# The one-hot matrices of near edges: VectorE's TENSOR_SCALAR comparisons written as TENSOR_TENSOR, in the last message pass of a graph network

## The chip, the cores and the metric

One core of a Trainium2 chip runs the whole program. The metric is the device time of one execution, in microseconds; the median of three runs of the kernel before is 5305.56 us (5305.24 to 5307.98).

## What is computed

A stack of four graph layers over 6250 nodes of 256 features and 100,000 edges; `dst` is sorted, `src` is random. Only the fourth layer, a graph convolution, matters here:

```python
h = jnp.maximum(_layernorm(x, axis=-1), 0.0)
# edge_index = stack([src, dst]); row = src, col = dst
dinv_sqrt = jnp.where(deg > 0, jax.lax.rsqrt(deg_safe), 0.0)
w = dinv_sqrt[row] * dinv_sqrt[col]
h = jax.ops.segment_sum(w[:, None] * x[col], row, num_segments=N)   # x here is the layer's input h
h = h @ W + b
return x + jnp.where(h >= 0, h, LEAKY_ALPHA * h)
```

The destinations are drawn as the square of a uniform number, so many edges point to the first nodes.

## The kernel before, in words

The nodes are in 49 buckets of 128 (NB). A message pass takes 128 edges at a time, a tile: POOL gathers 128 rows of a table in HBM by an indirect DMA (one instruction a tile), VectorE builds a one-hot matrix that says to which row of the bucket each edge belongs, and TensorE multiplies the matrix with the gathered rows and so sums them in PSUM.

The last pass is `bucket_pass` (L1539) with the name gcn. Its table `htab` holds the layer's input, already scaled. It treats edges in two ways. Edges whose `dst` is 640 or more ("rest") go by gathers, at most 12 tiles a bucket, 586 in all. Edges whose `dst` is one of the first 640 nodes ("near", DEEP = 5 blocks of 128) are not gathered: those 640 rows stay in SBUF (`rows`), and the pass counts how often each node of the bucket has an edge to each of them. For that, VectorE makes two one-hot matrices of each of at most 6 near tiles of a bucket, in `near_hot`: `hot_to` (L1609, 128 columns, which node of the bucket) and `hot_of` (L1610, 640 columns, which near row), 293 of each, written as bf16 from fp32 constants `iota` and `wide`. TensorE multiplies them in `near_sum` (L1664, up to 30 matmuls of 128x128, into `psA`), ScalarE copies the counts to `times` (L1639), and `near_product` (L1674) multiplies them with `rows` into the bucket's sum.

Each engine runs a list of its own, written out by hand; k is the place of a tile in its bucket b.

- POOL (L1591): gather t into slot t mod 16 of `got`, after the sum of tile t - 16 is done (`sums`).
- VectorE: the one-hot of the gathered tile 8 places ahead (L1601, `tensor_scalar`, fp32), then at k = 2 to 7 the near matrices of bucket b + 1 (one pair each), then the steps of the bucket before: at k = 8 `y` = product + bias (L1491, waits for TensorE's product of k = 6), at k = 9 the leaky slope (L1495), at k = 10 the sum with x (L1498).
- TensorE: the tile's matmul (L1682), after k = 1 `near_sum(b)`, after k = 6 `near_product(b)`; at k = 3 the transposes (L1526) and at k = 6 the product with the weights (L1532) of the bucket before.
- ScalarE: at k = 1 the scaled copy `a` of the finished bucket (L1508), at k = 3 `times` of bucket b, at k = 4 the copy of the transposes (L1512), at u = 11 the store of the result (L1515).

`near_hot(b)` waits for `near_sum(b - 2)` (two buffers); `near_sum(b)` waits for all near matrices up to bucket b (`near_hots`). Other lines that the text names: L765, in the attention pass (`edge_pass`), is a multiplication of VectorE with both inputs in SBUF, one of them broadcast along the free dimension; L1760 is the gather of the edge network, whose VectorE steps (L1783, L1802) have one input in PSUM; L577 scatters records and L1135 gathers them for the lists of edges.

Of the kernel before, what the change touches and what calls it, by code (L numbers as in the profile page):

```python
# [19 lines left out]
ALU = mybir.AluOpType  # L20
ACT = mybir.ActivationFunctionType
AX = mybir.AxisListType
P = 128
# [24 lines left out]
DEEP = 5  # L48
# [67 lines left out]
def wait_count(eng, sem, count):  # L116

    if count is not None and not (isinstance(count, int) and count <= 0):
        eng.wait_ge(sem, count)
# [1155 lines left out]
class Behind:  # L1275
# [10 lines left out]
    def sb(self, name, shape):  # L1286
        return self.st.enter_context(self.nc.sbuf_tensor(f"{name}_behind_{self.nm}", shape, F32))
# [4 lines left out]
    def sem(self, name):  # L1292
        return self.nc.alloc_semaphore(f"{name}_behind_{self.nm}")
# [245 lines left out]
def bucket_pass(nc, c, nm, table, row_of, rel_of, lay, behind, near=None):  # L1539
# [7 lines left out]
    with ExitStack() as st:  # L1547
# [8 lines left out]
        if near is not None:  # L1556
            to, of, rows_d = near
            layn = c.layouts["near"]
            first_near = [sum(layn.counts[0:b]) for b in range(NB + 1)]
            wide = sb("wide", [P, DEEP * P])  # L1560
            hot_to, hot_of = sb("hot_to", [P, 2, NEAR, P], BF16), sb("hot_of", [P, 2, NEAR, DEEP * P], BF16)
            times, rows = sb("times", [P, 2, DEEP, P]), sb("rows", [P, DEEP, D])
            psA = [[pt(f"psA{q}{h}") for h in range(2)] for q in range(2)]
            near_hots, near_sums, times_made, near_made, rows_in, widened = [sem(x) for x in (
                "near_hots", "near_sums", "times_made", "near_made", "rows_in", "widened")]
# [6 lines left out]
        @block.sync  # L1572
        def _(sp):
            if near is not None:
                sp.dma_start(rows[:, :, :], rows_d[0:DEEP * P, :].rearrange("(k p) d -> p k d", p=P)).then_inc(rows_in, 16)
                sp.wait_ge(rows_in, 16)
            for i in range(NB):
                after.keep(sp, i)
            after.sync_end(sp)
# [14 lines left out]
        @block.vector  # L1594
        def _(dve):
            def one_hot(t):

                if t >= lay.n:
                    return
                wait_count(dve, sums, t - U + 1)  # L1600
                nc.vector.tensor_scalar(hot[:, t % U, :], c.iota[:, :], rel_of[:, t:t + 1], None, ALU.is_equal).then_inc(hots, 1)  # L1601

            def near_hot(b, i):

                if near is None or b >= NB or not 0 <= i < layn.counts[b]:
                    return
                t = first_near[b] + i
                wait_count(dve, near_sums, b - 1)
                nc.vector.tensor_scalar(hot_to[:, b % 2, i, :], c.iota[:, :], to[:, t:t + 1], None, ALU.is_equal)  # L1609
                nc.vector.tensor_scalar(hot_of[:, b % 2, i, :], wide[:, :], of[:, t:t + 1], None, ALU.is_equal).then_inc(near_hots, 1)  # L1610

            after.vector_start(dve)
            if near is not None:
                dve.wait_ge(widened, 1)
                for i in range(NEAR):
                    near_hot(0, i)
            for t in range(HOT_LEAD):
                one_hot(t)
            for t, (b, k) in enumerate(where):
                one_hot(t + HOT_LEAD)  # L1620
                near_hot(b + 1, k - 2)
                if b:
                    after.vector(dve, b - 1, k)
                if k == lay.counts[b] - 1:
                    for u in range(k + 1, max(steps, U)):
                        if b:
                            after.vector(dve, b - 1, u)
            for u in range(max(steps, U)):
                after.vector(dve, NB - 1, u)
            after.vector_end(dve)  # L1630
# [1243 lines left out]
```

## Time and profile before

| | |
|---|---|
| median of three runs | 5305.56 us |
| the profiled execution, its span | 6597.1 us |
| TensorE busy (matmul) | 3895.4 us, 59% |
| VectorE busy | 2562.6 us, 39% |
| ScalarE busy | 1792.3 us, 27% |
| POOL busy | 3799.2 us, 58% |
| granted TensorE clock | 0.714 of full speed |
| last pass (gcn), in the profile | 5715 to 6597 us |

The profile is of one execution, whose time is its span; nothing is recorded around it. It is longer than every timed run: durations of single instructions and the order of events are read from it, and how they carry over to the runs has to be argued. Busy shares are means over stages with different limits, so each stage is read by itself.

### The profile page before, as it was taken

What the parts mean: (1) busy time and instruction counts of PE and PEld (TensorE: products, weight loads), DVE (VectorE), ACT (ScalarE), POOL (GpSimd) and SP (SyncE); (2) the same over time, 40 slices, a digit from 0 to 9 for tenths busy, and PEclk for the clock granted to TensorE, in tenths of its full rate; (3) what the DMA queues carried; (4) which work ended last, traced back from release to release, by engine and by line L of the source; (5) the groups of instructions that cost most, each with busy time, mean ns of one, the idle gap of its engine ahead of it and who ended that gap; (6) DMA issues with size and microseconds to landing.
All of it is one profiled execution on the core that took longest, in us unless ns stands there. A gap on an engine that the chain in (4) does not pass through costs nothing. (4 is left out here: it accounts for less than half of the span.)

```text
span 6597.1 us, 65618 instructions
## 1 busy us (share of the span) xinstructions
PE 3895.4 (59%) x14913; PEld 2594.0 (39%) x14914; DVE 2562.6 (39%) x8644; ACT 1792.3 (27%) x5648; POOL 3799.2 (58%) x3942
## 2 busy tenths in 40 slices
PE   4232666667641533596455555566777777577777
PEld 2121333333320510242333333355566555455555
DVE  4223444444430300132222222255555555644443
ACT  0111555555530400011000000044444444400000
POOL 3554666666666077402666666666666666277776
PEclk7565666766665765796676666667777777688888
DMA  1011332332310010144433333323333333233332
GB/s 48 20 41 60 88 88 87 89 89 87 88 45 3 0 42 22 59 148 141 124 99 98 98 98 98 96 82 87 87 87 86 87 86 89 77 98 99 99 98 87
DMA packets 277662, 527.83 MB, mean 80 GB/s; under 512 B 80566, under 2 KB 175259, under 8 KB 277049
## 3 DMA queue, kind: packets, MB, share of 16 engines
q0 software_dynamic: 176144, 422.24, 22.5%
q1 hardware_dynamic: 85200, 86.14, 3.9%
q10 hardware_dynamic: 15960, 15.41, 0.7%
q8 instruction: 137, 2.24, 0.1%
q14 instruction: 221, 1.81, 0.1%
HBM read 433.63 MB, written 89.82 MB: 79 GB/s over the span
## 5 line engine op out<-in xcount | busy, mean ns | idle before, releaser
L675 POOL DMA_INDIRECT got_attend_src_dst<-dram_gtab,gather_src x832 | 800.4, 962 | 531.0 <-DVE msg_attend_src_dst L747 320.9
L577 POOL DMA_INDIRECT dram_rec_src<-rec_src x784 | 766.5, 978 | 509.6 <-issue 243.5
L1760 POOL DMA_INDIRECT got_edge_mlp_src_dst<-dram_ptab,gather_src x832 | 786.3, 945 | 463.2 <-DVE pre_edge_mlp_src_dst L1802 252.9
L1591 POOL DMA_INDIRECT got_rgcn<-dram_xtab,gather_of_type x831 | 788.3, 949 | 392.5 <-issue 187.9
L1886 PE MATMUL psS_edge_mlp_src_dst<-msg_edge_mlp_src_dst,hot_edge_mlp_src_dst 128*128 128x256 f32 x1664 | 736.1, 568 | 434.0 <-DVE sage_sums L1783 223.6
L1591 POOL DMA_INDIRECT got_gcn<-dram_htab,gather_rest x586 | 616.5, 1052 | 234.1 <-issue 148.9
L861 PE MATMUL psS_attend_src_dst<-msg_attend_src_dst,hot_attend_src_dst 128*128 128x264 f32 x1664 | 700.8, 513 | 19.5 <-DVE msg_attend_src_dst L747 14.3
L2091 PE MATMUL psO_tab<-w_tab,hT_tab 128*128 128x512 f32 (+1 forms) x980 | 474.4, 633 | 350.1 <-issue 200.5
L1886 PEld LDWEIGHTS psS_edge_mlp_src_dst<-msg_edge_mlp_src_dst,hot_edge_mlp_src_dst 128*128 128x128 f32 x1664 | 388.5, 269 | 589.7 <-issue 338.8
L1682 PE MATMUL psS_rgcn<-got_rgcn,hot_rgcn 128*128 128x257 f32 x1662 | 543.8, 471 | 79.7 <-DMA got_rgcn<-dram_xtab,gather_of_type 55.0
L1783 DVE TENSOR_TENSOR sage_sums<-sage_sums,psS_edge_mlp_src_dst 128x256 f32 x832 | 347.8, 418 | 523.6 <-PE psS_edge_mlp_src_dst L1886 246.1
L884 PE MATMUL psF_attend_src_dst<-ident,hot_attend_src_dst 128*128 128x128 f32 x832 | 314.4, 378 | 356.2 <-ACT hotT_attend_src_dst L832 190.4
L877 PEld LDWEIGHTS psN_attend_src_dst<-node,hotT_attend_src_dst 128*128 128x128 f32 x1664 | 412.5, 253 | 138.1 <-issue 41.4
L1682 PEld LDWEIGHTS psS_rgcn<-got_rgcn,hot_rgcn 128*128 128x128 f32 x1662 | 362.8, 234 | 237.3 <-issue 169.2
L2091 PEld LDWEIGHTS psO_tab<-w_tab,hT_tab 128*128 128x128 f32 x980 | 199.3, 215 | 573.1 <-issue 409.3
L1850 ACT ACTIVATE msg_edge_mlp_src_dst<-pre_edge_mlp_src_dst 128x256 f32<-128x256 f32 x832 | 340.3, 413 | 293.8 <-DVE pre_edge_mlp_src_dst L1802 211.3
L1802 DVE TENSOR_TENSOR pre_edge_mlp_src_dst<-got_edge_mlp_src_dst,psE_edge_mlp_src_dst 128x256 f32<-128x256 f32 x832 | 344.4, 414 | 158.4 <-remote 104.1
L709 DVE TENSOR_TENSOR sums<-sums,psS_attend_src_dst 128x264 f32 x832 | 350.7, 422 | 64.8 <-issue 31.5
L861 PEld LDWEIGHTS psS_attend_src_dst<-msg_attend_src_dst,hot_attend_src_dst 128*128 128x128 f32 x1664 | 361.1, 266 | 37.2 <-DVE msg_attend_src_dst L747 30.7
L1601 DVE TENSOR_SCALAR hot_rgcn<-iota,rel_src 128x128 f32<-128x128 f32 x831 | 216.9, 315 | 390.4 <-remote 180.5
L2067 DVE COPY out_tab<-psO_tab 128x512 f32<-128x512 f32 x196 | 133.7, 690 | 588.4 <-DMA got_edge_mlp_src_dst<-dram_ptab,gather_src 308.9
L1682 PE MATMUL psS_gcn<-got_gcn,hot_gcn 128*128 128x257 f32 x1172 | 322.8, 409 | 64.8 <-issue 30.8
(397 smaller groups left out, 5878.7 us busy)
## 6 DMA issues: line engine op xcount, KB each, us to landing
dram_xtab<-out_tab SPq DMA_DIRECT2D x48, 1024.0 KB
got_edge_mlp_src_dst<-dram_ptab,gather_src POOLq DMA_INDIRECT x832
got_attend_src_dst<-dram_gtab,gather_src POOLq DMA_INDIRECT x832
got_rgcn<-dram_xtab,gather_of_type POOLq DMA_INDIRECT x831
dram_rec_src<-rec_src POOLq DMA_INDIRECT x784
got_gcn<-dram_htab,gather_rest POOLq DMA_INDIRECT x586
dram_gtab<-sums ACTq DMA_DIRECT2D x48, 132.0 KB
x_sb<-x_in SPq DMA_DIRECT2D x1, 6144.0 KB
```

Of the source, the lines that this page charges most:

```text
L577: nc.gpsimd.indirect_dma_start(edges.to, bass.IndirectOffsetOnAxis(edges.rec[:, column, PLACE:PLACE + 1].bitcast(I32), 0), edges.rec[:, co ...
L675: nc.gpsimd.indirect_dma_start(got[:, t % U, 0:w], None, table, bass.IndirectOffsetOnAxis(row_of[:, t:t + 1], 0)).then_inc(row_in[t % U], 16)
L709: nc.vector.tensor_tensor(here, here, psS[t[1] % banks][:, 0:cols], ALU.add).then_inc(added, 1)
L861: nc.tensor.matmul(psS[t[1] % banks][:, 0:cols], hot[:, t[1], :], rows(t), start=True, stop=True).then_inc(sums, 1)
L877: nc.tensor.matmul(psN[t[1] // 2 % 2][:, 2 * HEADS * (t[1] % 2):2 * HEADS * (t[1] % 2 + 1)], hotT[:, t[1] % 4, :], c.node[:, :, :].rearran ...
L1591: nc.gpsimd.indirect_dma_start(got[:, t % U, 0:D], None, table, bass.IndirectOffsetOnAxis(row_of[:, t:t + 1], 0)).then_inc(row_in[t % U], 16)
L1682: nc.tensor.matmul(psS[b % 2][:, 0:D + 1], hot[:, t % U, :], got[:, t % U, 0:D + 1], start=(k == 0), stop=(k == lay.counts[b] - 1), skip_g ...
L1760: nc.gpsimd.indirect_dma_start(got[:, t % U, 0:width], None, table, bass.IndirectOffsetOnAxis(row_of[:, t:t + 1], 0)).then_inc(row_in[t % ...
L1783: nc.vector.tensor_tensor(here, here, psS[t[1] % banks][:, 0:cols], ALU.add).then_inc(added, 1)
L1802: nc.vector.tensor_tensor(pre[:, t[1] % 4, :], got[:, t[1], 0:D], psE[t[1] % 4][:, 0:D], ALU.add).then_inc(pres, 1)
L1886: nc.tensor.matmul(psS[t[1] % banks][:, 0:cols], hot[:, t[1], :], msg[:, t[1] % 8, :], start=True, stop=True).then_inc(sums, 1)
L2091: last = nc.tensor.matmul(psO[(NBK * t[1] + b) % 4][:, 0:z - a], hT[:, t[1], k * P:(k + 1) * P], w[:, k, a:z], start=(k == 0), stop=(k == 1))
```

## The change

In `near_hot` both comparisons become `tensor_tensor` with the column of indices broadcast along the free dimension. The values are the same; sizes, types, order, waits and the semaphore stay. The one-hot of the gathered tiles (L1601) stays a `tensor_scalar`.

```diff
--- before.py
+++ after.py
@@ -1606,8 +1606,9 @@
                     return
                 t = first_near[b] + i
                 wait_count(dve, near_sums, b - 1)
-                nc.vector.tensor_scalar(hot_to[:, b % 2, i, :], c.iota[:, :], to[:, t:t + 1], None, ALU.is_equal)
-                nc.vector.tensor_scalar(hot_of[:, b % 2, i, :], wide[:, :], of[:, t:t + 1], None, ALU.is_equal).then_inc(near_hots, 1)
+                nc.vector.tensor_tensor(hot_to[:, b % 2, i, :], c.iota[:, :], to[:, t:t + 1].to_broadcast([P, P]), ALU.is_equal)
+                nc.vector.tensor_tensor(hot_of[:, b % 2, i, :], wide[:, :], of[:, t:t + 1].to_broadcast([P, DEEP * P]),
+                                        ALU.is_equal).then_inc(near_hots, 1)
 
             after.vector_start(dve)
             if near is not None:
```

## Rows read from the trace of the kernel before

**Rows 1.** The last stage: length, busy PE, PEld, DVE, ACT, POOL, clock, DMA, GB/s.
```profile
5715.00:6597.00 882.00, 635.11 (x3421) 496.99 (x3421) 366.97 (x1319) 75.53 (x196) 617.23 (x588) 0.83 0.32 96
```

**Rows 2.** Groups by line in 5715 to 6597: busy us, mean ns, idle before.
```profile
L1591 POOL DMA_INDIRECT got_gcn<-dram_htab,gather_rest x586 | 616.5, 1052 | 234.1 <-issue 148.9 <-PE psS_gcn L1682 42.9 <-DMA got_attend_src_dst<-dram_gtab,gather_src 42.3
```

**Rows 3.** Groups by line of the whole span, POOL's; then POOL's longest single wait.
```profile
L675 POOL DMA_INDIRECT got_attend_src_dst<-dram_gtab,gather_src x832 | 800.4, 962 | 531.0 <-DVE msg_attend_src_dst L747 320.9 <-issue 190.7 <-POOLq L2751 19.4
L1591 POOL DMA_INDIRECT got_rgcn<-dram_xtab,gather_of_type x831 | 788.3, 949 | 392.5 <-issue 187.9 <-PE psS_rgcn L1682 102.4 <-remote 101.6
L1760 POOL DMA_INDIRECT got_edge_mlp_src_dst<-dram_ptab,gather_src x832 | 786.3, 945 | 463.2 <-DVE pre_edge_mlp_src_dst L1802 252.9 <-issue 210.3
L577 POOL DMA_INDIRECT dram_rec_src<-rec_src x784 | 766.5, 978 | 509.6 <-issue 243.5 <-POOLq L2751 211.5 <-PEq L1943 37.5
...
POOL rows_order_whole L1135 <- SPq L1117: 320.0, 1, 320.0
```

**Rows 4.** The timeline of one bucket: start us, us, engine, line, idle before.
```profile
6103.23 1.84 PE L1664 MATMUL psA_gcn<-hot_to_gcn,hot_of_gcn 128*128 128x128 bf16 x30
6103.24 0.29 DVE L1601 TENSOR_SCALAR hot_gcn<-iota,rel_rest 128x128 f32<-128x128 f32 x1
6103.44 0.28 DVE L1609 TENSOR_SCALAR hot_to_gcn<-iota,rel_near 128x128 bf16<-128x128 f32 x1
6103.63 0.54 DVE L1610 TENSOR_SCALAR hot_of_gcn<-wide_gcn,near_dst 128x640 bf16<-128x640 f32 x1
6103.78 1.44 POOL L1591 DMA_INDIRECT got_gcn<-dram_htab,gather_rest  x1 [0.31 <-issue]
6104.10 0.28 DVE L1601 TENSOR_SCALAR hot_gcn<-iota,rel_rest 128x128 f32<-128x128 f32 x1
...
6105.53 1.41 POOL L1591 DMA_INDIRECT got_gcn<-dram_htab,gather_rest  x1 [0.30 <-issue]
...
6112.05 0.76 ACT L1639 COPY times_gcn<-psA_gcn 128x512 f32<-128x512 f32 x2 [9.01 <-remote]
6112.33 0.94 POOL L1591 DMA_INDIRECT got_gcn<-dram_htab,gather_rest  x1 [1.35 <-DMA got_attend_src_dst<-dram_gtab,gather_src]
...
6112.86 4.11 PE L1674 MATMUL psS_gcn<-rows_gcn,times_gcn 128*128 128x256 f32 x10 [2.98 <-issue]
...
6116.81 1.03 PE L1532 MATMUL psO_behind_gcn<-w,aT_behind_gcn 128*128 128x256 f32 x4
...
6117.67 3.20 PE L1682 MATMUL psS_gcn<-got_gcn,hot_gcn 128*128 128x257 f32 x14
6117.87 0.42 DVE L1491 TENSOR_TENSOR y_behind_gcn<-psO_behind_gcn,bias 128x256 f32<-128x256 f32 x1 [10.08 <-issue]
...
6118.40 0.42 DVE L1495 SCALAR_TENSOR_TENSOR z_behind_gcn<-y_behind_gcn 128x256 f32<-128x256 f32 x1
6118.58 1.07 POOL L1591 DMA_INDIRECT got_gcn<-dram_htab,gather_rest  x1 [0.30 <-PE psS_gcn L1682]
6118.74 0.28 DVE L1601 TENSOR_SCALAR hot_gcn<-iota,rel_rest 128x128 f32<-128x128 f32 x1
...
6120.70 1.84 PE L1664 MATMUL psA_gcn<-hot_to_gcn,hot_of_gcn 128*128 128x128 bf16 x30
```

**Rows 5.** The waits in 5715 to 6597; then one window of PE's near_product.
```profile
ACT times_gcn L1639 <- remote: 348.5, 44, 17.6
...
6112.86:6117.00 4.14, 4.14 (x11) 3.37 (x12) 0.00 (x0) 0.22 (x1) 3.23 (x4) 0.59 0.30 93
```

**Rows 6.** The attention pass: VectorE's L765 by line, then the timeline.
```profile
L765 DVE TENSOR_TENSOR sums<-sums,own 128x1792 f32<-128x1792 f32 x7 | 13.6, 2018 | 2.3 <-issue 2.3
...
4308.60 3.95 DVE L765 TENSOR_TENSOR sums<-sums,own 128x1792 f32<-128x1792 f32 x2
4309.80 1.64 POOL L675 DMA_INDIRECT got_attend_src_dst<-dram_gtab,gather_src  x1 [0.30 <-issue]
```

## The prediction, made before the changed kernel was run

> **What bounds the kernel now.** I read the stages first, then the fourth pass by line, then one bucket of it in order of time.
>
> Stages [rows 1]: the change touches the last stretch alone, 5715 to 6597 us, 882 us for 49 buckets and 586 gathers. POOL is busy there for 617 us and PE for 635, DVE for only 367. So VectorE has slack, and its longer work costs nothing by itself; what counts is what it does to POOL.
>
> By line [rows 2]: in this pass a gather takes 1052 ns on average. In the relational pass the same instruction takes 949 and in the edge network 945 [rows 3]. The excess is 586 x 0.107 = 63 us, and no PE or DMA row explains it.
>
> In order of time [rows 4]: a gather with VectorE quiet takes 0.94 us and the next one starts 0.30 later, a spacing of 1.25. While VectorE makes near matrices they take 1.44 and 1.41. The second value repeats, since VectorE goes round a step of three comparisons in 0.854 (6103.24 to 6104.10), and a gather with its gap takes two such steps, 1.71 (6103.78 to 6105.53 is 1.75, the one before it not yet in step). So POOL and VectorE exclude each other somewhere, and POOL loses. Beside L1495, too, a gather takes 1.07.
>
> What else waits: PE's 30 near_sum matmuls are over by 6105.07, yet ScalarE, which waits for their semaphore alone, copies at 6112.05. PE sits idle at near_product for 3 us meanwhile, and POOL, 16 tiles ahead, idles 1.35 instead of 0.30 [rows 4]. One bucket's loop there is PE's: 8.8 from near_sum's first matmul to the copy, 0.8 copy, 4.1 near_product, 1.0 product, 3.2 for seven tiles, some of it overlapped, and near_sum starts again 17.5 us after it did. No operation of the program accounts for those 7 us, and `remote` is all that the view of the waits names for them, 348 us in the pass [rows 5]. The span is 6597.1 and the median of the runs 5305.56, 20% less. I take the late semaphore for something of the profiled execution. POOL's own spacing must be shorter in the runs as well: 832 + 832 + 831 + 586 + 784 = 3865 such instructions x 1.25 = 4831 us, and with two waits in which POOL does nothing (320 us at L1135, 212 at L577) this is 5363, over the median [rows 3]. So in the runs a gather's spacing s is below 1.25; it is not under 0.945, what the instruction itself takes. **I choose** s of 1.0 to 1.2, and POOL as the bound of the pass: 12 gathers per bucket are 12 to 14.4 us, while PE's work with prompt semaphores is 12 tiles x 0.457 (seven take 3.20) + 1.8 for near_sum + 4.1 for near_product, or half of that at full clock (it ran at a granted 0.59 [rows 5]), + 1.7 for the two products of the bucket before = 11 to 13.
>
> **The change part by part.** It replaces 293 comparisons of 128 columns and 293 of 640, one for one; no semaphore, queue or DMA moves.
> - VectorE's time. TENSOR_SCALAR: 0.196 from start to start for 128 columns, 0.463 for 640, so 0.52 ns a column over 0.13. TENSOR_TENSOR: 256 columns take 0.418 with the next start after 0.336 [rows 4], 1792 columns 2.018 with the next after 1.93 [rows 6], so 1.04 ns a column over 0.07. Two fp32 inputs in SBUF thus cost 0.20 for 128 columns and 0.736 for 640 (durations about 0.285 and 0.82). The step grows from 0.854 to D = 0.196 + 0.202 + 0.736 = 1.134, VectorE's busy time by 293 x 0.28 = 82 us. The cover: VectorE idles 10 us per bucket before L1491 [rows 4], the burst of six steps grows by 1.7, and the near matrices are due a bucket later. If a bucket takes 13 us in the runs there are still some 4 us. I cost it at nothing; without cover it is those 82 us.
> - POOL's loss today: 63 us of excess in the profile, less 49 x 0.12 = 6 for the gather of 1.07: 57 us, 1.2 per bucket. With a shorter spacing the same burst costs between that and three gathers x (1.71 - s), 2.1 at s = 1.0.
> - POOL's loss afterwards. No row shows a 640-column TENSOR_TENSOR beside this gather. Lowest bound: none, as beside additions that read PSUM, where the 832 gathers of the edge network average 945. Upper bound: the gather stands still as it does now, for the longer 0.736. The nearest row is L765 [rows 6], a multiplication with two SBUF inputs, 2.02 us each. A gather started at 4309.80 under one that ran from 4308.60 to 4310.62, and ended at 4311.44, 0.82 after it: its normal 0.95 counted from 0.13 before its end. So such an instruction does hold a gather **that wants to start**, until about 0.13 before its recorded end. The next L765 had begun at 4310.53 and did not stop it again. That is the difference from today, where a gather is stopped at its start and again later, by the next 640-column comparison. From this I price the new loss: at a random moment the start waits (0.82 - 0.13)^2 / (2 x 1.134) = 0.21, with the short comparisons 0.23; a burst of 6.8 us holds 4.6 gathers at s = 1.25, 1.06 us per bucket, 52 us in all. If s is under 1.134, the gathers fall in step with VectorE, one a step, and lose 6 x (1.134 - s): 0.2 at s = 1.1, 0.8 at 1.0.
> - The sum. s = 1.25: 57 - 52 = 5 us won. s = 1.1: 3 x 0.61 = 1.8 before, 0.2 after, 1.6 per bucket, 78 us. s = 1.0: 1.0 (out of step, like now) to 2.1 before against 0.8, so 0.2 to 1.3 per bucket, 10 to 64 us. Not all of it reaches the end, since PE's loop is close behind. I take 0.5 us per bucket, 49 x 0.5 = **25 us**. Against the profile's own 6597.1 the same terms give 5 us, and there PE's late loop hides them; a profile after within 10 us of that span would not contradict me.
>
> The Trainium skill, SBUF — State Buffer, "Who interferes with whom", says that a two-port VectorE instruction shuts GpSimd out, that tensor_tensor with two SBUF inputs contends only with GpSimd instructions that read SBUF, and infers that descriptor generation, which writes, is not held by it. By that all 57 us would come back. The gather of 1.64 us [rows 6] speaks against it for the start and for it afterwards.
>
> **The rivals.**
> - *Nothing that can be measured* (within 0.2%, 10.6 us, about what a measurement of this kernel can tell). Either s is near 1.2, where the two losses are alike, or PE's loop bounds the runs as it does the profile: then POOL's relief becomes a longer wait for sums. For: the 1.35 idle and the 17.5 us loop. Against: the loop needs the 7 us semaphore delay. 5300 to 5306.
> - *Full relief*: TENSOR_TENSOR does not hold the gathers at all. For: the 945 of the edge network. Against: [rows 6]. All 57 us: 5249.
> - *Slower*: the longer hold outweighs the second stop. Place: the start of each gather in a burst. Price: 6 x (D - s) per bucket against 1.0 to 1.2 now. It decides from D - s of 0.2, so with s near 1.0 if the comparisons' overhead is the 0.13 of TENSOR_SCALAR (D = 1.26) and not 0.07: 1.5 against 1.0, 0.5 x 49 = 25 us, 5331.
> - *The change does nothing to the instruction*: the broadcast column could be taken as a scalar again. L765 has such an operand and stands in the trace as TENSOR_TENSOR at 1.04 ns a column [rows 6]; I count this with the first rival, at 5306.
>
> **How the numbers follow.** Forecast 0.42, nothing measurable 0.28, full relief 0.09, slower 0.21. Time: 5305.6 - 25 = 5281. Range: down to the sum at s = 1.1 less a few us, 5232; up to most of the slower case, 5325. Both signs hold much of the chance; the forecast's own range is 5232 to 5294. Faster 0.42 + 0.09 = 0.51, same 0.28, slower 0.21.
>
> **What the profile after would show.** Right: L1609 and L1610 as TENSOR_TENSOR of about 285 and 820 ns, a step of 1.13, a mean gather under 1052 but over 945, with its excess in gathers that start under a L1610 and none in those that start just after one. Wrong: a mean of 945 (full relief), or over 1052 (slower); an idle before L1491 near zero, which would make VectorE the bound; or gathers relieved and POOL's wait for sums grown by as much, which would make it PE's pass.

## The result and the profile after

The changed kernel takes 5362.63 us (median of 4 runs, 5361.77 to 5363.98) against 5306.25 of the kernel before in the same session: a ratio of 1.0104 with a 95% interval of 1.009 to 1.0119, 56 us slower. The forecast was 25 us faster, with a range that ended at 5325.

First, the profile shown ahead of the prediction has to be set right. The profile of the changed kernel spans 5360.1 us, what its runs take. The kernel before, profiled once more (experiment e1), spans 5313.6 and not 6597.1. The first profile was of a disturbed execution. What its instructions take on VectorE and POOL was true all the same; what it showed of TensorE's late semaphores was not of this kernel. The comparison below is therefore of the profile after with the second profile of before.

The kernel before, second profile: the first line of the page, POOL's group of the last pass, the last pass as one window (length, busy PE, PEld, DVE, ACT, POOL, clock, DMA share, GB/s), and its longest waits.

```profile
span 5313.6 us, 65614 instructions
...
L1591 POOL DMA_INDIRECT got_gcn<-dram_htab,gather_rest x586 | 619.6, 1057 | 178.5 <-issue 97.7 <-PE psS_gcn L1682 80.8
...
4495.00:5313.00 818.00, 617.21 (x3421) 451.29 (x3421) 366.02 (x1319) 78.43 (x196) 620.36 (x588) 0.93 0.34 103
...
PE psS_gcn L1682 <- DMA got_gcn<-dram_htab,gather_rest: 130.3, 207, 1.7
```

The same of the changed kernel, with the page's line of engines.

```profile
span 5360.1 us, 65614 instructions
...
PE 3836.6 (72%) x14909; PEld 2402.2 (45%) x14914; DVE 2673.2 (50%) x8644; ACT 1795.6 (33%) x5648; POOL 3860.8 (72%) x3942
...
L1591 POOL DMA_INDIRECT got_rgcn<-dram_xtab,gather_of_type x831 | 789.8, 950 | 253.4 <-issue 159.6
...
L1591 POOL DMA_INDIRECT got_gcn<-dram_htab,gather_rest x586 | 673.6, 1150 | 178.4 <-issue 112.3 <-PE psS_gcn L1683 66.1
...
4489.00:5360.00 871.00, 649.94 (x3421) 487.64 (x3421) 444.94 (x1319) 78.44 (x196) 674.38 (x588) 0.87 0.33 97
...
PE psS_gcn L1683 <- DMA got_gcn<-dram_htab,gather_rest: 176.2, 173, 2.0
```

In both profiles POOL's idle time in the pass is 178 us, and that is no wait: 586 x 0.30 us between two gathers. It is 178 us in the profile of every experiment below too, whatever TensorE and VectorE did there. So POOL never waits for another engine there; it **is** the pass. Its busy time grew from 619.6 to 673.6, by 54 us, the pass by 53, the run by 56. TensorE waits for the gathers' data, 130 us before and 176 after; the mean granted clock of the pass is 0.93 before and 0.87 after, and since POOL does not wait for TensorE, that is not what made the pass longer. The relational pass, whose gathers took 949 ns before [rows 3], is at 950: the loss is all in the last pass.

VectorE's side of it, the changed kernel by line (busy us, mean ns, idle before):

```profile
L1610 DVE TENSOR_TENSOR hot_of_gcn<-wide_gcn,near_dst 128x640 bf16<-128x640 f32 x293 | 237.8, 812 | 0.0
...
L1609 DVE TENSOR_TENSOR hot_to_gcn<-iota,rel_near 128x128 bf16<-128x128 f32 x293 | 81.5, 278 | 6.4 <-POOL wide_gcn L1585 6.4
L1491 DVE TENSOR_TENSOR y_behind_gcn<-psO_behind_gcn,bias 128x256 f32<-128x256 f32 x49 | 20.8, 425 | 412.6 <-PE psO_behind_gcn L1532 412.6
```

The comparisons cost what was forecast, and VectorE still idles 413 us before L1491, 8.4 per bucket. Its own time is not the bound.

One burst in order of time. The changed kernel, POOL and then VectorE (start us, us):

```profile
4932.39 1.03 POOL L1591 DMA_INDIRECT got_gcn<-dram_htab,gather_rest  x1 [0.30 <-PE psS_gcn L1683]
4933.72 1.96 POOL L1591 DMA_INDIRECT got_gcn<-dram_htab,gather_rest  x1 [0.30 <-PE psS_gcn L1683]
4935.99 1.96 POOL L1591 DMA_INDIRECT got_gcn<-dram_htab,gather_rest  x1 [0.30 <-PE psS_gcn L1683]
4938.25 1.02 POOL L1591 DMA_INDIRECT got_gcn<-dram_htab,gather_rest  x1 [0.30 <-PE psS_gcn L1683]
4939.58 0.95 POOL L1591 DMA_INDIRECT got_gcn<-dram_htab,gather_rest  x1 [0.30 <-issue]
...
4935.91 0.28 DVE L1601 TENSOR_SCALAR hot_gcn<-iota,rel_rest 128x128 f32<-128x128 f32 x1
4936.11 0.28 DVE L1609 TENSOR_TENSOR hot_to_gcn<-iota,rel_near 128x128 bf16<-128x128 f32 x1
4936.31 0.82 DVE L1610 TENSOR_TENSOR hot_of_gcn<-wide_gcn,near_dst 128x640 bf16<-128x640 f32 x1
4937.05 0.28 DVE L1601 TENSOR_SCALAR hot_gcn<-iota,rel_rest 128x128 f32<-128x128 f32 x1
```

The kernel before, second profile, POOL in a burst:

```profile
4910.81 1.48 POOL L1591 DMA_INDIRECT got_gcn<-dram_htab,gather_rest  x1 [0.30 <-PE psS_gcn L1682]
4912.59 1.40 POOL L1591 DMA_INDIRECT got_gcn<-dram_htab,gather_rest  x1 [0.30 <-issue]
4914.30 1.25 POOL L1591 DMA_INDIRECT got_gcn<-dram_htab,gather_rest  x1 [0.31 <-issue]
4915.85 0.95 POOL L1591 DMA_INDIRECT got_gcn<-dram_htab,gather_rest  x1 [0.30 <-issue]
```

The gather of 4935.99 starts just after a one-hot (L1601, 4935.91) has begun. It ends at 4937.95, 0.82 after the end of the 640-column comparison (4937.13), which is the distance that L765 had shown [rows 6]. It began under the one-hot and was let in neither where L1609 began nor where L1610 did. Then the next gather comes 2.27 us after it started, which is two of VectorE's steps (2 x 1.133), **at the same place of the step**, and is lost in the same way. Before, a lost gather with its gap took 1.71, two steps of 0.854. Both kernels run in such a lock; in the new one each turn of it costs 1.02 us instead of 0.46. Counted over the whole trace of the changed kernel, 100 gathers took more than 1.65 us, 52 of them right behind another such one, and they hold 99 of the 120 us that POOL loses.

### The profile page after: what moved, and what is told of

Its sections match the earlier page's. It is cut to its first block and busy times, and to the rows that moved or that the text cites. A ratio compares the mean times of both kernels' runs of the same rounds, so it can differ in the third digit from the quotient of the medians.

```text
span 5360.1 us, 65614 instructions
## 1 busy us (share of the span) xinstructions
PE 3836.6 (72%) x14909; PEld 2402.2 (45%) x14914; DVE 2673.2 (50%) x8644; ACT 1795.6 (33%) x5648; POOL 3860.8 (72%) x3942
## 5 line engine op out<-in xcount | busy, mean ns | idle before, releaser
L1683 PE MATMUL psS_rgcn<-got_rgcn,hot_rgcn 128*128 128x257 f32 x1662 | 757.9, 558 | 232.0 <-DMA got_rgcn<-dram_xtab,gather_of_type 195.8
L1887 PE MATMUL psS_edge_mlp_src_dst<-msg_edge_mlp_src_dst,hot_edge_mlp_src_dst 128*128 128x256 f32 x1664 | 676.4, 528 | 242.8 <-DVE sage_sums L1784 160.2
L1591 POOL DMA_INDIRECT got_gcn<-dram_htab,gather_rest x586 | 673.6, 1150 | 178.4 <-issue 112.3
L861 PE MATMUL psS_attend_src_dst<-msg_attend_src_dst,hot_attend_src_dst 128*128 128x264 f32 x1664 | 616.8, 457 | 86.9 <-DVE msg_attend_src_dst L747 80.1
L1683 PE MATMUL psS_gcn<-got_gcn,hot_gcn 128*128 128x257 f32 x1172 | 365.1, 429 | 224.0 <-DMA got_gcn<-dram_htab,gather_rest 176.2
L877 PEld LDWEIGHTS psN_attend_src_dst<-node,hotT_attend_src_dst 128*128 128x128 f32 x1664 | 340.0, 217 | 172.2 <-issue 113.5
L2092 PE MATMUL psO_tab<-w_tab,hT_tab 128*128 128x512 f32 (+1 forms) x980 | 398.1, 554 | 2.5 <-DVE out_tab L2066 1.9
L1683 PEld LDWEIGHTS psS_gcn<-got_gcn,hot_gcn 128*128 128x128 f32 x1172 | 208.3, 201 | 333.3 <-DVE hot_gcn L1601 167.9
L861 PEld LDWEIGHTS psS_attend_src_dst<-msg_attend_src_dst,hot_attend_src_dst 128*128 128x128 f32 x1664 | 301.6, 225 | 121.8 <-DVE msg_attend_src_dst L747 119.1
L747 DVE TENSOR_TENSOR msg_attend_src_dst<-got_attend_src_dst,msg_attend_src_dst 128x256 f32<-128x256 f32 x832 | 346.4, 416 | 0.7 <-issue 0.7
L1601 DVE TENSOR_SCALAR hot_rgcn<-iota,rel_src 128x128 f32<-128x128 f32 x831 | 218.5, 305 | 242.7 <-PE psS_rgcn L1683 241.9
```

The costliest lines, as they stand in the source:

```text
L747: nc.vector.tensor_tensor(msg[:, t[1] % 8, 0:D].rearrange("p (h d) -> p h d", d=DH), got[:, t[1], 0:D].rearrange("p (h d) -> p h d", d=DH) ...
L861: nc.tensor.matmul(psS[t[1] % banks][:, 0:cols], hot[:, t[1], :], rows(t), start=True, stop=True).then_inc(sums, 1)
L1591: nc.gpsimd.indirect_dma_start(got[:, t % U, 0:D], None, table, bass.IndirectOffsetOnAxis(row_of[:, t:t + 1], 0)).then_inc(row_in[t % U], 16)
L1683: nc.tensor.matmul(psS[b % 2][:, 0:D + 1], hot[:, t % U, :], got[:, t % U, 0:D + 1], start=(k == 0), stop=(k == lay.counts[b] - 1), skip_g ...
L1887: nc.tensor.matmul(psS[t[1] % banks][:, 0:cols], hot[:, t[1], :], msg[:, t[1] % 8, :], start=True, stop=True).then_inc(sums, 1)
L2092: last = nc.tensor.matmul(psO[(NBK * t[1] + b) % 4][:, 0:z - a], hT[:, t[1], k * P:(k + 1) * P], w[:, k, a:z], start=(k == 0), stop=(k == 1))
```

## The experiments

All are edits of the last pass alone. "Excess" is POOL's: 586 gathers x (their mean - 0.945 us), from POOL's group in each profile. "Step" is the time from one near pair of VectorE's burst to the next, the median of each trace. Differences are medians against the kernel before in the same session.

| run | edit | step, us | mean gather, ns | excess, us | time, us | ratio (95% interval) |
|---|---|---|---|---|---|---|
| e1 | before, again | 0.854 | 1057 | 66 | 5315.3 | |
| change | both TENSOR_TENSOR | 1.133 | 1150 | 120 | +56 | 1.0104 (1.009 to 1.0119) |
| e2 | only L1609 | 0.860 | 1048 | 60 | -5 | 0.9991 (0.9982 to 1.0001) |
| e3 | only L1610 | 1.127 | 1078 | 78 | +14 | 1.0029 (1.0017 to 1.004) |
| e4 | both and L1601 | 1.140 | 1319 | 219 | +162 | 1.0306 (1.0288 to 1.0323) |
| e5 | output as 5 x 128 | 0.854 | 1054 | 64 | +1 | 1.0001 (0.9992 to 1.0011) |
| e6 | change, pause ahead of the pair | 1.330 | 978 | 19 | -45 | 0.9911 (0.9895 to 0.9928) |
| e7 | before, pauses ahead and behind | 1.248 | 958 | 8 | -57 | 0.9891 (0.9874 to 0.9907) |
| e8 | before, 16-bit constants | 0.654 | 960 | 9 | -56 | 0.9889 (0.9873 to 0.9906) |
| e9 | change, two fillers, two inputs | 1.304 | 982 | 22 | -41 | 0.9918 (0.9901 to 0.9934) |
| e10 | change, a filler with one input | 1.326 | 987 | 25 | -40 | 0.9923 (0.9906 to 0.9939) |
| e11 | change, pause behind the pair | 1.257 | 957 | 7 | -60 | 0.9886 (0.9869 to 0.9902) |
| e12 | e7 with 16-bit constants | 0.993 | 952 | 4 | -61 | 0.9883 (0.9867 to 0.99) |
| e13 | change, one filler | 1.250 | 956 | 6 | -58 | 0.9891 (0.9874 to 0.9907) |
| e14 | e4, pause ahead of the pair | 1.333 | 989 | 26 | -42 | 0.9921 (0.9904 to 0.9937) |
| e15 | change, five fillers | 1.518 | 1097 | 89 | +25 | 1.0044 (1.0027 to 1.0061) |

Read down the columns of excess and time: the time follows the excess less 66 us within 10 us everywhere, over a range of more than 220 us. The step alone does not give the excess: e3, the change and e4 have steps of 1.127 to 1.140 us and lose 78, 120 and 219 us. Whatever VectorE was made to do, with up to 1.5 us per step instead of 0.85, only what POOL lost counted.

**e1, the kernel before once more.**

> The kernel before, unchanged, for a second profile, since the first one spans 6597 us against runs of 5306 while the profile of the changed kernel spans 5360 against runs of 5363. If the first profile was of a disturbed execution: a span near 5305, near_sum's semaphore at ScalarE within 2 us of the last matmul, a gather's spacing beside a quiet VectorE still 1.25 us, and a mean gather of the last pass near 1.05 us. If profiling itself slows this kernel: a span near 6600 again.

Its span is 5313.6 us. TensorE's near_sum and ScalarE's copy behind it:

```profile
4912.91 1.84 PE L1664 MATMUL psA_gcn<-hot_to_gcn,hot_of_gcn 128*128 128x128 bf16 x30
...
4914.79 0.75 ACT L1639 COPY times_gcn<-psA_gcn 128x512 f32<-128x512 f32 x2 [3.74 <-PE psA_gcn L1664]
```

The copy starts as the matmuls end, where the first profile had 7 us between them. The gathers' spacing beside a quiet VectorE is 1.25 us here too, so that was no effect of the disturbance.

**e2 to e4, which of the comparisons does it.** Each line is as in the change or as before; e4 also turns L1601:

```diff
-nc.vector.tensor_scalar(hot[:, t % U, :], c.iota[:, :], rel_of[:, t:t + 1], None, ALU.is_equal).then_inc(hots, 1)
+nc.vector.tensor_tensor(hot[:, t % U, :], c.iota[:, :], rel_of[:, t:t + 1].to_broadcast([P, P]), ALU.is_equal).then_inc(hots, 1)
```

> Only the 128-column comparison of each pair is a TENSOR_TENSOR; the 640-column one stays TENSOR_SCALAR. Theory A (POOL's gathers are held by the long two-input comparison, each for up to a whole step of VectorE): the long one is back at 0.46 us, so the time is within 10 us of before, the gathers' mean near 1.05 us. Theory B (VectorE's own time is what came through): within 3 us of before. Theory C (any two-input comparison between two-port ones shuts the gather out, whatever its length): slower than before by 20 to 60 us.

> Only the 640-column comparison is a TENSOR_TENSOR. Theory A: most of the 57 us comes back, +45 to +65 us over before, gathers of 1.9 to 2.0 us in the bursts. Theory B: VectorE's busy time rises by 80 us of the full 82, so +55 us, but with VectorE idle before L1491 near zero. Theory C: the gather now has a two-port comparison on both sides of the long one and gets in once a step, as today: within 20 us of before.

> The one-hot of the gathered tiles in the last pass (L1601, 586 of 128 columns) is a TENSOR_TENSOR too, so no two-port instruction is left in the bursts. Theory A with the price of my prediction (the gather waits only for the instruction in flight when it wants to start): the loss falls to about 1 us per bucket, so the time returns to within 10 us of before. Theory A', the gather can enter only at the end of the 640-column comparison: +50 to +60 us as in the change. Theory B: VectorE does 4 us more than in the change, so +57 to +61 us. Theory C: the gathers get in at every end of an instruction once no two-port one is there: within 10 us of before or faster.

e2 changes nothing that matters, as A had it; theory C, which wanted 20 to 60 us more, fails there, though its range for e3 (within 20 us) came true. e3, where VectorE's work grows by nearly as much as in the change (step 1.127 against 1.133), costs 14 us and not 45 to 65: VectorE's time is not it (B), and not the long comparison by itself (A as I had put it). Its seven runs lie 23 us apart, and the profiled one is the shortest of them, so here the excess and the median match only roughly. Its gathers alternate, 1.02 and 1.75, in a lock of another kind: 3.39 us from the first to the third is three steps, for two gathers. It loses 0.88 us in three steps where the change loses 1.02 in two:

```profile
4907.71 1.02 POOL L1591 DMA_INDIRECT got_gcn<-dram_htab,gather_rest  x1 [0.31 <-issue]
4909.04 1.75 POOL L1591 DMA_INDIRECT got_gcn<-dram_htab,gather_rest  x1 [0.30 <-issue]
4911.10 1.02 POOL L1591 DMA_INDIRECT got_gcn<-dram_htab,gather_rest  x1 [0.30 <-issue]
```

e4 missed every forecast, by 100 us and more. Its profile has gathers that stand still for a whole burst; the last comparison of that burst is the second row:

```profile
4986.48 7.68 POOL L1591 DMA_INDIRECT got_gcn<-dram_htab,gather_rest  x1 [0.30 <-PE psS_gcn L1685]
...
4993.05 0.28 DVE L1602 TENSOR_TENSOR hot_gcn<-iota,rel_rest 128x128 f32<-128x128 f32 x1
```

It ends at 4994.16, again 0.83 after the last comparison (4993.33). So a gather that waits is not served at the next boundary between two instructions as a rule; 17 boundaries went by. Of e4's gathers 28 took 7.3 us or more, at most one in a burst, and they hold 191 of its 219 us. This is no lock of two periods but a gather kept out until the burst is over.

**e5, a slower form with one input.**

```diff
-nc.vector.tensor_scalar(hot_of[:, b % 2, i, :], wide[:, :], of[:, t:t + 1], None, ALU.is_equal).then_inc(near_hots, 1)
+nc.vector.tensor_scalar(hot_of[:, b % 2, i, :].rearrange("p (a q) -> p a q", a=DEEP), wide[:, :], of[:, t:t + 1], None, ALU.is_equal).then_inc(near_hots, 1)
```

> The kernel before, with the output of the 640-column TENSOR_SCALAR written as 5 x 128 where its input is one run of 640, meant to take it out of the mode that reads and writes two columns at once: about 0.8 us of VectorE each, one input, no second port. VectorE's time is then that of the change, without its second input. Theory A (POOL's gathers are what is held, by a two-input or two-port instruction): the mean gather falls under 1.06 us, the time is 0 to 45 us under before. Theory B (VectorE's time): slower by about 50 us like the change. If the comparison stays at 0.54 us the edit did nothing and the run says nothing.

L1610 stayed at 544 ns, so the edit did nothing and the run says nothing. A form of that length that leaves POOL alone was not found.

**e6 to e8, pauses and shorter comparisons.** e6 adds a wait to the change, e7 that wait and one behind the pair to the kernel before; e8 changes the constants of the kernel before to 16 bits:

```diff
+                if after_tile is not None:
+                    dve.wait_ge(hots, min(after_tile + HOT_LEAD + 1, lay.n))     # e6, e7: ahead of the pair
...
+                dve.wait_ge(near_hots, t + 1)                                    # e7, e11: behind it
...
-            wide = sb("wide", [P, DEEP * P])
+            wide = sb("wide", [P, DEEP * P], mybir.dt.float16)                   # e8, e12
...
-                nc.vector.tensor_scalar(hot_to[:, b % 2, i, :], c.iota[:, :], to[:, t:t + 1], None, ALU.is_equal)
+                nc.vector.tensor_scalar(hot_to[:, b % 2, i, :], c.iota_bf[:, :], to[:, t:t + 1], None, ALU.is_equal)
```

> The changed kernel, with VectorE waiting for its own one-hot (L1601, the two-port comparison) to finish before each pair of near comparisons, so some 0.1 us of nothing stand between them. Theory D, from the traces so far: a gather that wants to start under the two-port comparison is passed over when a two-input comparison follows without a gap, and again at the next one, until the 640-column one ends (1.96 us instead of 0.95). With a gap it gets in there: gathers of 1.96 vanish, the loss falls from 2.4 to about 0.7 to 1.2 us per bucket, 50 to 85 us under the changed kernel, 0 to 30 under before. Theory A' (only the end of the 640-column comparison lets it in): the gathers stay at 1.9 or longer, the time at the change's or a little over. Theory B (VectorE's time): slower than the change by 293 x 0.1 = 30 us.

> The kernel before, with VectorE waiting for its own last comparison ahead of each near pair and behind it, so POOL finds the port free twice in a step. Theory D: the gathers of 1.40 and 1.48 us fall to under 1.25, and up to 30 of the 66 us lost in the bursts come back. Theory B: slower by up to 2 x 293 x 0.1 = 59 us. If gaps in VectorE's stream do nothing for POOL: within 5 us of before.

> The kernel before with 16-bit constants (column numbers as fp16 for the 640-column comparison, which holds them exactly, and bf16 for the 128-column one), so that both near comparisons have 16-bit data on both sides. If that doubles their rate, as 16-bit data do for L404 (784 columns in 0.36 to 0.38 us), the 640-column one takes about 0.38 us and the other 0.24, the step falls from 0.854 to about 0.65. Theory A: shorter holds, the loss of 1.2 to 1.3 us per bucket falls to 0.5 to 1.0, 15 to 40 us under before, unless the gathers fall in step with two or three of the shorter steps. Theory B: within 5 us of before or faster by no more than VectorE's 60 us.

All three are faster than the kernel before, by 45 to 57 us, and each won more than was expected of it (up to 30 us for e6 and e7, 15 to 40 for e8). e6 is the change with 0.2 us more per step and takes 100 us less than it. That seemed to bear out theory D, that a gather needs a gap behind the one-hot (L1601). In e8 the 640-column comparison takes 376 ns and the step 0.654.

**e9 to e12, the gap against the length of the step.**

```diff
+nc.vector.tensor_tensor(spare[:, b % 2, i, 0:16], c.iota[:, 0:16], to[:, t:t + 1].to_broadcast([P, 16]), ALU.is_equal)   # e13 one, e9 two, e15 five (8 columns)
...
+nc.vector.tensor_reduce(spare[:, b % 2, i, :], c.iota[:, :], AX.X, ALU.max)      # e10
```

> The changed kernel with two more comparisons of 16 columns, two inputs in SBUF each, between the one-hot and each near pair, without a gap. The step of VectorE grows from 1.13 by about 0.2 us, as in the kernel with the pause (1.33), which took the gathers from 1.96 to 1.03 us. Theory D (what lets a gather in is the free port behind the two-port one-hot): no gap, so the gathers still take 1.9 us and more, and the time is at the changed kernel's or above, +50 to +100 us over before. Theory P (the pause helped only because a step of 1.33 and a gather's spacing of 1.25 fall in step): within 20 us of the kernel with the pause, 35 to 55 under before.

> The changed kernel with a reduction of 128 columns (one input in SBUF, no second port) between the one-hot and each near pair: VectorE is busy there, but leaves the shared port alone for about 0.2 us. Theory D: as good as the pause, gathers near 1.03 us and 30 to 55 us under before. If a gather needs VectorE to have drained, not only the port: no better than the changed kernel, +50 to +80. Theory P: as with the pause too, so it is told from D by the other filler.

> The changed kernel with VectorE waiting for the 640-column comparison to finish behind each pair, none ahead of it. Theory D: in the changed kernel's trace a gather gets in at that place already, and is passed over between the one-hot and the 128-column comparison, where there is still no gap; so the loss stays near 2 us per bucket, the time within 30 us of the changed kernel's, above before. Theory P or any gap will do: 30 to 55 us under before.

> The kernel before with 16-bit constants and with VectorE's waits ahead of and behind each near pair. Either alone left 7 to 9 us of the 66 us that POOL lost in this pass, so little is left: POOL's excess 2 to 9 us, 57 to 65 us under before, and within 8 us of either alone. If POOL were no longer the bound: no gain over either.

Theory D, as the only way out, falls twice. e9 has no gap anywhere, only more two-input comparisons, and is 41 us faster than before, 97 faster than the change. e11 has its pause where the changed kernel served gathers already, and is better than e6. e10, with the one-input filler, is 40 us faster than before, as both D and P had it, so it does not tell them apart. What e6, e9, e10 and e11 share is the step: 1.25 to 1.33, where the change has 1.133. In e11 the step has come to the gathers' own spacing, and each gather meets VectorE at the same harmless place:

```profile
4886.58 0.96 POOL L1591 DMA_INDIRECT got_gcn<-dram_htab,gather_rest  x1 [0.30 <-issue]
4887.84 0.95 POOL L1591 DMA_INDIRECT got_gcn<-dram_htab,gather_rest  x1 [0.30 <-PE psS_gcn L1684]
4889.09 0.95 POOL L1591 DMA_INDIRECT got_gcn<-dram_htab,gather_rest  x1 [0.30 <-PE psS_gcn L1684]
...
4886.84 0.82 DVE L1610 TENSOR_TENSOR hot_of_gcn<-wide_gcn,near_dst 128x640 bf16<-128x640 f32 x1
...
4888.09 0.82 DVE L1610 TENSOR_TENSOR hot_of_gcn<-wide_gcn,near_dst 128x640 bf16<-128x640 f32 x1
```

But the step is not all of it, and D is not dead. The traces can be counted at the one place where most of the change's losses begin: gathers that start 62 to 73 ns after a one-hot did, with a near pair or its filler next.

| run | what follows the one-hot | gathers that start at this place | held for over 1.65 us in all |
|---|---|---|---|
| change | L1609 as TENSOR_TENSOR, at once | 83 | 83 |
| e4 | the same, behind a TENSOR_TENSOR one-hot | 28 | 7 |
| e3 | L1609 as TENSOR_SCALAR, at once | 23 | 0 |
| e10 | the filler with one input, at once | 52 | 0 |
| e6 | a pause | 18 | 0 |
| e14 | a pause, behind a TENSOR_TENSOR one-hot | 38 | 0 |
| e9, e11, e13, e15 | two-input fillers; in e11 L1609 | 3 (e11) | 0 |

So where a gather does come to the bad place, a pause or a one-input instruction behind the one-hot lets it in, as D had it (e6, e10, e14). In e9 and e11, and in e13 and e15 below, hardly any gather comes there: in e11 the nearest ones start 77 to 83 ns after a one-hot with L1609 next, 19 of them, and take 1.02 us at most. A few nanoseconds are enough: of the change's own 17 gathers that start 74 to 92 ns after, 5 are held. As far as these counts go, the step decides how often gathers come to a bad place, and the comparisons around it decide what that costs.

e12 joins e7 and e8; with POOL's excess at 4 us there is nothing left to win here. It is the fastest, with e11 within 2 us of it.

**e13 to e15, the step's length as a forecast.**

> The changed kernel with one more comparison of 16 columns ahead of each near pair, no gap: VectorE's step 1.22 us. Theory P (the step's length against the gathers' 1.25 decides): the gathers slide through the step by 0.03 us each and at most one a burst meets the bad place, so POOL's excess is 10 to 60 us (the changed kernel 120, the kernel before 66), the time 5 to 60 us under before. Theory H (a short two-input instruction right behind the one-hot is what cures it, whatever the step): the same as with two fillers, 40 us under before within 10. If 0.09 us more of VectorE's work does nothing: +50 us over before.

> All three comparisons of the last pass as two-input instructions (step 1.14 us, 162 us slower than before, single gathers of up to 9.4 us), with VectorE waiting ahead of each near pair (step about 1.33). Theory P: the gathers fall in step, one a step, and lose about 0.08 each, no long stops: POOL's excess under 40 us, the time 20 to 50 us under before. Theory T (two-input instructions one behind the other keep a waiting gather out for as long as they come, and the pause lets it in once a step): long stops vanish, but a gather can still be held from one pause to the next, up to 1.2 us: excess 60 to 120 us, before's time or up to 60 over.

> The changed kernel with five more comparisons of 8 columns ahead of each near pair, no gap: VectorE's step about 1.53 us. Theory P: the gathers fall in step, one a step, each losing the step less 1.25, about 0.28, six to a burst: 1.7 us per bucket, POOL's excess 70 to 95 us, the time 5 to 30 us over before, gathers of about 1.23 us in the bursts. Theory H: 40 us under before. If VectorE's time counts: it does 2 us per bucket more than in the changed kernel, so +100 us and more over before.

e15 is the sharpest of them: more of the same filler that won 41 us in e9 now loses 25, excess 89 us, within the forecasts of 5 to 30 and 70 to 95. The gathers are in step, one to a step of 1.52:

```profile
4900.71 1.21 POOL L1592 DMA_INDIRECT got_gcn<-dram_htab,gather_rest  x1 [0.30 <-PE psS_gcn L1689]
4902.23 1.22 POOL L1592 DMA_INDIRECT got_gcn<-dram_htab,gather_rest  x1 [0.30 <-issue]
4903.75 1.21 POOL L1592 DMA_INDIRECT got_gcn<-dram_htab,gather_rest  x1 [0.30 <-issue]
...
4901.81 0.81 DVE L1616 TENSOR_TENSOR hot_of_gcn<-wide_gcn,near_dst 128x640 bf16<-128x640 f32 x1
...
4903.33 0.81 DVE L1616 TENSOR_TENSOR hot_of_gcn<-wide_gcn,near_dst 128x640 bf16<-128x640 f32 x1
```

e13's time is in its range (58 us under before), its excess of 6 a little better than the 10 to 60 expected: the step came out at 1.250 and not the 1.22 that I had added up, so it too runs at the gathers' pace. H, which wanted e9's time, is off by 17 us, and VectorE's work explains nothing of it. e14 shows that with two-input comparisons alone, too, nearly all of the loss can go: at a step of 1.333 the excess is 26 us and the long stops of e4 are gone, within P's ranges and not T's. But it changes both the pause and the step of e4, and no run gave e4 a filler in place of the pause, so which of the two ended the long stops is open.

## Why the prediction was wrong, point by point

- *VectorE's time*: right. 812 and 278 ns for 0.82 and 0.285, a step of 1.133 for 1.134, and no cost by itself: the idle before L1491 is 413 us.
- *POOL bounds the pass*: right, and stronger than put. Its idle is nothing but its fixed 0.30; nothing of POOL's loss was hidden, and TensorE's loop was not close behind.
- *The spacing s of 1.0 to 1.2*: wrong. It is 1.25 in the runs as in the profile. I had argued it down from 3865 gathers x 1.25 plus two waits being over the median, but the two waits were of the disturbed profile: 320 and 212 us there, 11 and 20 us in e1. With s = 1.25 my own sum gave 5 us, not 25; the 25 rested on the shorter spacing. The two waits in e1 (us, times, longest):

```profile
POOL dram_rec_src L577 <- POOLq L2751: 20.3, 3, 8.2
...
POOL rows_order_whole L1135 <- SPq L1117: 11.0, 1, 11.0
```
- *Today's loss*: 57 us forecast for the bursts, 66 us in all in e1. Right.
- *The loss afterwards*: the step that failed. I priced each gather as one that wants to start "at a random moment" and waits for the one comparison then in flight, 0.23 us each, 52 us in all. Two things were missing. A gather that waits can be passed over at the next boundary, and was so here through L1601, L1609 and L1610, 1.02 us. And the moments are not random: the lost gather and its gap make 2.27 us, two steps, so the next one is lost too, as long as the burst lasts. POOL's excess came to 120 us against 52. Why a gather is passed over stays open. I had used the same lock for the kernel before (1.71 = 2 x 0.854), and for the new one only below s = 1.134.
- *The rival "slower"* (0.21) had the right sign and place, the start of each gather in a burst, but not the price: its formula 6 x (D - s) gives nothing at s = 1.25 and D = 1.133. That formula holds for steps longer than the spacing: at e15's 1.518 it gives 1.6 us per bucket, 79 us, for 89 measured.
- *Full relief*, where the Trainium skill's page SBUF — State Buffer, "Who interferes with whom", led: that page says that a two-input tensor_tensor contends with GpSimd instructions that read SBUF, and infers that writing descriptors is not stopped by it. Here the start of a gather is stopped, 1.02 us at a time in the changed kernel and 6.7 us in e4. The gather also reads its indices, `gather_rest`, from SBUF, which the prediction left out of account: whether that read is what is held, as the page's first statement would have it, no run here shows. The page also has the loser wait until the other's instruction is finished; the gather of e4 shown above was kept out through 18.

## What to carry to other kernels

Where POOL issues indirect DMAs back to back and VectorE runs a periodic stream beside it, compare the period with the gathers' spacing before pricing anything: in the changed kernel the two lengths fell in step at a place where a gather is held, and 0.12 us more of work per step turned 56 us lost into 58 won. The period alone is no price, though: at about 1.13 us three mixes of comparisons lost 78, 120 and 219 us. Waits of VectorE for its own results, or 16-bit constants that shorten the comparisons, got back 56 to 61 of the 66 us that the kernel before lost too. And when a profile's span is not the time of the runs, profile again before using its waits.

## What the runs showed of the hardware that was not expected

- A gather that is waiting can be kept out by a gapless stream of two-input VectorE instructions until the stream ends: 7.68 us in one case of e4, 9.36 at the longest. Why it is let in at some boundaries and passed over at others is not settled. What follows the one-hot matters (83 of 83 lost in the change, none of 52 in e10, at the same place), and so do hundredths of a microsecond in the gather's start; e4 passes over 7 of 28 at one and the same place.
- An instruction of POOL that takes 0.946 us undisturbed never starts closer than 1.24 us to the last (1.25 in the median), in every pass and every run here.
- Splitting a contiguous output into 5 x 128 did not change how VectorE ran the comparison (544 ns for 541).
